# The last frame of a gated graph network: candidate product ahead of the update gate, the final update in pieces

## What is computed

```
a  = adj @ h                                   # in_mat and out_mat are both adj
z  = sigmoid([a, a] @ w3.T + b3 + h @ u3.T + bu3)
r  = sigmoid([a, a] @ w4.T + b4 + h @ u3.T + bu3)
hv = tanh([a, a] @ w5.T + b5 + (r * h) @ u5.T + bu5)
h  = (1 - z) * h + z * hv                      # three times
out = layernorm(x + h)                         # mean and variance over 256 features, no weights
```

## Time and profile before

| what | value |
|---|---|
| median of 3 runs | 763.11 us (762.76 to 763.23) |
| the profiled execution | 762.16 us |
| its span, first to last instruction | 760.4 us |
| PE busy | 747.4 us, 98% |
| DVE, ACT, POOL busy | 544.6 (72%), 388.3 (51%), 72.7 us (10%) |
| mean granted TensorE clock | 0.995 |

### The profile page before, as it was taken

The page is one execution under the profiler, slowest core; times in us unless marked ns, Lnnn a source line. Parts: engine busy times, 40 slices in busy tenths (PEclk is TensorE's granted clock), DMA queues, the critical chain, the costliest instruction groups (busy, mean ns, idle before and its releaser), DMA issues.

```text
span 760.4 us, 10506 instructions
## 1 busy us (share of the span) xinstructions
PE 747.4 (98%) x3696; PEld 633.4 (83%) x3696; DVE 544.6 (72%) x858; ACT 388.3 (51%) x647; POOL 72.7 (10%) x91
## 2 busy tenths in 40 slices
PE   9999999999999999999999999999999999999994
PEld 8888888888888888888888888888888888888883
DVE  5666787677767776787677766887677756887675
ACT  4545544455556453554556544545466545444454
POOL 0000021100110011110100001120000000211003
PEclk9999999999999999999999999999999999999998
DMA  8122411224453322223355332221335432212222
GB/s 308 29 38 38 91 29 31 38 41 87 114 121 65 88 58 35 37 38 58 66 121 119 85 91 32 38 35 30 68 64 130 128 67 37 32 31 32 42 39 112
DMA packets 208445, 52.15 MB, mean 69 GB/s; under 512 B 201232, under 2 KB 201360, under 8 KB 208400
## 3 DMA queue, kind: packets, MB, share of 16 engines
q1 hardware_dynamic: 208112, 51.23, 31.2%
q10 hardware_dynamic: 288, 0.27, 0.1%
HBM read 18.95 MB, written 8.39 MB: 36 GB/s over the span
## 4 chain that ended last, share of the span: by engine, by line
PE 98%; DVE 1%; ACT 0%; POOL 0%; issue 0%; ACTq 0%; POOLq 0%
PE ps_g L323 17%; PE ps_g L324 17%; PE ps_g L325 17%; PE ps_v L325 11%; PE ps_v L324 11%; PE ps_v L323 11%; PE ps_a L348 11%; PE ps_g L406 1%; DVE dz L609 0%; DVE hT L619 0%; DVE dz L604 0%; DVE hT_lo L635 0%; PE ps_a L445 0%; DVE stats L717 0%; POOL rstd L751 0%
## 5 line engine op out<-in xcount | busy, mean ns | idle before, releaser
L484 ACT ACTIVATE ps_v<-ps_v,bias 128x512 f32<-128x512 f32 x96 | 63.6, 663 | 200.3 <-PE ps_v L325 200.3
L325 PE MATMUL ps_g<-aT_hi,wt_hi 128*128 128x512 f32 x384 | 149.4, 389 | 0.0
L323 PE MATMUL ps_g<-aT_hi,wt_lo 128*128 128x512 f32 x384 | 149.4, 389 | 0.0
L324 PE MATMUL ps_g<-aT_lo,wt_hi 128*128 128x512 f32 x384 | 149.4, 389 | 0.0
L604 DVE TENSOR_TENSOR dz<-ps_v,hT 128x512 f32<-128x512 f32 x64 | 44.3, 692 | 103.6 <-ACT ps_v L484 103.6
L514 ACT CAST rh_hi<-rh 128x512 fp32r<-128x512 f32 x96 | 59.5, 620 | 78.2 <-DVE rh L624 78.2
L519 ACT ACTIVATE z<-ps_g,bias 128x512 f32<-128x512 f32 x96 | 64.2, 686 | 48.6 <-PE ps_g L325 48.6
L323 PEld LDWEIGHTS ps_g<-aT_hi,wt_lo 128*128 128x128 f32 x384 | 72.1, 188 | 15.0
L324 PEld LDWEIGHTS ps_g<-aT_lo,wt_hi 128*128 128x128 f32 x384 | 72.1, 188 | 15.0
L325 PEld LDWEIGHTS ps_g<-aT_hi,wt_hi 128*128 128x128 f32 x384 | 72.1, 188 | 14.9
L599 DVE TENSOR_TENSOR aT_lo<-ps_a,aT_hi 128x512 fp32r<-128x512 f32 x96 | 62.5, 674 | 28.8 <-ACT aT_hi L471 28.7
(11 more groups left out here) (60 smaller groups left out, 1169.1 us busy)
## 6 DMA issues: line engine op xcount, KB each, us to landing
hn<-hb SPq DMA_DIRECT2D x736, 32.0 KB, 2.0
x_in<-in_x_rows SPq DMA_DIRECT2D x16, 512.0 KB, 4.9
xT<-in_x_cols SPq DMA_DIRECT2D x15, 512.0 KB, 4.4
out<-y SPq DMA_DIRECT2D x15, 512.0 KB, 2.7
wide<-in_w_t SPq DMA_DIRECT2D x3, 512.0 KB, 6.2
xT<-in_x_cols SPq DMA_DIRECT2D x2, 256.0 KB, 4.3
out<-y SPq DMA_DIRECT2D x2, 256.0 KB, 2.0
square<-in_u_t ACTq DMA_DIRECT2D x1, 256.0 KB, 2.8
```

The costliest lines, as they stand in the source:

```text
L323: nc.tensor.matmul(dst, lhs_lo, rhs_hi, start=first, stop=False, skip_group_check=True)
L324: nc.tensor.matmul(dst, lhs_hi, rhs_lo, start=False, stop=False, skip_group_check=True)
L325: return nc.tensor.matmul(dst, lhs_hi, rhs_hi, start=False, stop=last, skip_group_check=True)
L484: nc.scalar.activation(ps_v[:, oc, :], ps_v[:, oc, :], ACT.Tanh, bias=bias[:, BV, oc:oc + 1]).then_inc(v_ready, 1)
```

## The change

In the last frame alone the order of work is another. PE runs the transposes of slot 2 right after `value`, then `candidate`, and `gate_z` last; to make that possible `gate_z` of frame 11 leaves `second_half`, and in the loop over rounds it stands at the head of the next pass. The update of frame 11 takes v-h of both chunks first; chunk 0 of z, of the product and of the sum stays whole, chunk 1 is made in two halves of 256 rows (two batches each). The transposes of slot 3 go by chunk and half, batches 0 and 1 into a bank of `ps_g[0]`, batch 2 and batch 3 into a bank of `ps_v` each. Slot 3 has an output tile of its own (`y_tail`); ACT scales batches 0, 1 and 2, DVE scales batch 3 by one `tensor_scalar`. The statistics of slot 1 come after those of slot 2 on DVE, and its scaling and its store after those of slot 2. On ACT z of the last frame comes after the first two batches of slot 2.

```diff
--- before.py
+++ after.py
@@ -114,6 +114,7 @@
         hb = [sb(f"hb{k}", [P, C, GB, QUADS, BLK]) for k in range(2)]
         z = [sb(f"z{k}", [P, C, ROWS]) for k in range(2)]
         y = [sb(f"y{k}", [P, GB, D]) for k in range(2)]
+        y_tail = sb("y_tail", [P, GB, D])
 
 
         hT_hi = sb("hT_hi", [P, C, ROWS], F32R)
@@ -190,6 +191,10 @@
         zd_ready = sem("zd_ready")
         h_ready = sem("h_ready")
 
+        tail_zpre, tail_z, tail_zd, tail_h = sem("tail_zpre"), sem("tail_z"), sem("tail_zd"), sem("tail_h")
+        tail_normed = [sem(f"tail_normed{hf}") for hf in range(2)]
+        tail_stored = sem("tail_stored")
 
 
         pool_passed, dve_passed = sem("pool_passed"), sem("dve_passed")
@@ -226,6 +231,14 @@
 
         def weight(k):
             return square[k - U3] if k in (U3, U5) else wsum[k]
+        def y_bank(q, b):
+            if q == SLOTS - 2:
+                return by_batch(ps_a[:, b // HB, :])[:, b % HB, :]
+            if b < HB:
+                return by_batch(ps_g[0][:, 0, :])[:, b, :]
+            return ps_v[:, b - HB, 0:D]
 
         block = ctx.enter_context(nc.Block())
 
@@ -305,15 +318,16 @@
             last = ROUNDS - 1
             for j in range(EARLY, FR - 1):
                 frame(last, j, True, False)
-            for q in range(SLOTS - 1):
+            for q in (0, 2, 1):
                 store(last, q)
             for hf in range(2):
                 part = slice(hf * HB, (hf + 1) * HB)
-                sp.wait_ge(normed[SLOTS - 1], GB * last + HB * (hf + 1))
+                sp.wait_ge(tail_normed[hf], HB)
                 sp.dma_start(out_rows[:, B - GB + hf * HB:B - GB + (hf + 1) * HB, :],
-                             y[1][:, part, :]).then_inc(stored[1], DMA)
+                             y_tail[:, part, :]).then_inc(tail_stored, DMA)
             sp.wait_ge(stored[0], DMA * (SLOTS // 2 * ROUNDS + 1))
-            sp.wait_ge(stored[1], DMA * (SLOTS // 2 * ROUNDS + 2))
+            sp.wait_ge(stored[1], DMA * (SLOTS // 2 * ROUNDS))
+            sp.wait_ge(tail_stored, DMA * 2)
 
 
         @block.tensor
@@ -387,7 +401,8 @@
 
                 gate_r(i, j)
                 value(i, j, carry)
-                gate_z(i, j)
+                if j < FR - 1:
+                    gate_z(i, j)
 
             def candidate(i, j):
 
@@ -431,6 +446,7 @@
 
             first_round()
             with nc.Fori(1, ROUNDS, engines=(pe.engine,), hint_back_edge=True) as i:
+                gate_z(i - 1, FR - 1)
                 first_half(i, 0, True)
                 candidate(i - 1, FR - 1)
                 for j in range(FR):
@@ -448,15 +464,29 @@
                         done.then_inc(y_transposed, 1)
 
             last = ROUNDS - 1
+            def last_output(c, hf):
+                for b in range(hf * HB, (hf + 1) * HB):
+                    done = nc.tensor.transpose(y_bank(SLOTS - 1, b)[:, c * P:(c + 1) * P],
+                                               hT[SLOTS - 1][:, c, b * N:(b + 1) * N], ident[:, :])
+                if c == C - 1:
+                    done.then_inc(y_transposed, 1)
             pe.wait_ge(a_lo_ready, 2 * frames(last, FR - 1))
             for c in range(C):
                 pe.wait_ge(h_ready, C * frames(last, FR - 2) - 1 + c)
                 output(SLOTS - 2, c, ps_a)
             candidate(last, FR - 1)
+            gate_z(last, FR - 1)
             pe.wait_ge(z_ready, C * frames(last, FR - 2))
-            for c in range(C):
-                pe.wait_ge(h_ready, C * frames(last, FR - 1) - 1 + c)
-                output(SLOTS - 1, c, ps_g[0])
+            pe.wait_ge(d_ready, C * frames(last, FR - 1))
+            pe.wait_ge(tail_h, 1)
+            for hf in range(2):
+                last_output(0, hf)
+            for hf in range(2):
+                pe.wait_ge(tail_h, hf + 2)
+                last_output(1, hf)
 
 
         @block.scalar
@@ -554,9 +584,22 @@
                 for j in range(FR - 1):
                     frame(i, j, True, (i, j + 1))
             last = ROUNDS - 1
-            frame(last, FR - 1, False, None)
-            tanh_v(last, FR - 1)
-            normalise(last, 1)
+            j = FR - 1
+            tanh_v(last, j - 1)
+            normalise(last, 0)
+            for oc in range(C):
+                act.wait_ge(rpre_ready, C * frames(last, j) - 1 + oc)
+                nc.scalar.activation(r_sb[:, oc, :], ps_g[1][:, oc, :], ACT.Sigmoid,
+                                     bias=bias[:, BR, oc:oc + 1]).then_inc(r_ready, 1)
+            for oc in range(C):
+                act.wait_ge(rh_ready, C * frames(last, j) - 1 + oc)
+                nc.scalar.copy(rh_hi[:, oc, :], rh[:, oc, :]).then_inc(rh_hi_ready, 1)
+            tanh_v(last, j)
+            def last_z(oc, rows):
+                act.wait_ge(zpre_ready, C * frames(last, j) - 1 + oc)
+                nc.scalar.activation(z[1][:, oc, rows], ps_g[1][:, oc, rows], ACT.Sigmoid,
+                                     bias=bias[:, BZ, oc:oc + 1]).then_inc(tail_z, 1)
 
             q = SLOTS - 2
             act.wait_ge(shift_ready[q], ROUNDS)
@@ -564,13 +607,18 @@
             for b in range(GB):
                 nc.scalar.activation(y[0][:, b, :], by_batch(ps_a[:, b // HB, :])[:, b % HB, :], ACT.Identity,
                                      bias=shift[q][:, b:b + 1], scale=rstd[q][:, b:b + 1]).then_inc(normed[q], 1)
+                if b == 1:
+                    last_z(0, slice(0, ROWS))
+                    for hf in range(2):
+                        last_z(1, slice(hf * HALF, (hf + 1) * HALF))
+            normalise(last, 1)
             q = SLOTS - 1
-            act.wait_ge(stored[1], DMA * turn(last, q))
-            for hf in range(2):
+            for hf, batches in enumerate(((0, 1), (2,))):
                 act.wait_ge(shift_ready[q], last + 1 + hf)
-                for b in range(hf * HB, (hf + 1) * HB):
-                    nc.scalar.activation(y[1][:, b, :], by_batch(ps_g[0][:, hf, :])[:, b % HB, :], ACT.Identity,
-                                         bias=shift[q][:, b:b + 1], scale=rstd[q][:, b:b + 1]).then_inc(normed[q], 1)
+                for b in batches:
+                    nc.scalar.activation(y_tail[:, b, :], y_bank(q, b), ACT.Identity,
+                                         bias=shift[q][:, b:b + 1], scale=rstd[q][:, b:b + 1])\
+                      .then_inc(tail_normed[hf], 1)
 
 
         @block.vector
@@ -708,26 +756,53 @@
                 for j in range(FR - 1):
                     frame(i, j, True, (i, j + 1))
             last = ROUNDS - 1
-            frame(last, FR - 1, True, None)
-
-            def last_statistics(q, src, hf):
+            j = FR - 1
+            v_minus_h(last, j - 1, 0)
+            times_z(last, j - 1, 0)
+            v_minus_h(last, j - 1, 1)
+            new_h(last, j - 1, 0)
+            times_z(last, j - 1, 1)
+            new_h(last, j - 1, 1)
+            for c in range(C):
+                times_r(last, j, c)
+            rh_low(last, j, 0)
+            rh_low(last, j, 1)
+            def last_statistics(q, hf):
 
                 dve.wait_ge(y_transposed, 2 * (q - (SLOTS - 2)) + hf + 1)
                 for b in range(hf * HB, (hf + 1) * HB):
-                    nc.vector.bn_stats(stats[q][:, b, :],
-                                       by_batch(src[:, hf, :])[:, b % HB, :]).then_inc(stats_ready[q], 1)
+                    nc.vector.bn_stats(stats[q][:, b, :], y_bank(q, b)).then_inc(stats_ready[q], 1)
                 dve.wait_ge(stats_ready[q], GB * last + HB * (hf + 1))
                 for b in range(hf * HB, (hf + 1) * HB):
                     nc.vector.bn_aggr(meanvar[q][:, b, :], stats[q][:, b, :]).then_inc(meanvar_ready[q], 1)
 
-            last_statistics(SLOTS - 2, ps_a, 0)
-            last_statistics(SLOTS - 2, ps_a, 1)
+            for hf in range(2):
+                last_statistics(SLOTS - 2, hf)
+            statistics(last, 1)
             for c in range(C):
-                v_minus_h(last, FR - 1, c)
-                times_z(last, FR - 1, c)
-                new_h(last, FR - 1, c)
-            last_statistics(SLOTS - 1, ps_g[0], 0)
-            last_statistics(SLOTS - 1, ps_g[0], 1)
+                v_minus_h(last, j, c)
+            def last_h(c, rows, nth):
+                dve.wait_ge(d_ready, C * frames(last, j) - 1 + c)
+                dve.wait_ge(tail_z, nth)
+                nc.vector.tensor_tensor(dz[:, c, rows], dz[:, c, rows], z[1][:, c, rows], ALU.mult).then_inc(tail_zd, 1)
+                dve.wait_ge(tail_zd, nth)
+                dve.wait_ge(xh_ready[SLOTS - 1], last + 1)
+                nc.vector.tensor_tensor(hT[SLOTS - 1][:, c, rows], dz[:, c, rows], xT[SLOTS - 1][:, c, rows],
+                                        ALU.add).then_inc(tail_h, 1)
+            last_h(0, slice(0, ROWS), 1)
+            for hf in range(2):
+                last_h(1, slice(hf * HALF, (hf + 1) * HALF), hf + 2)
+            q = SLOTS - 1
+            for hf in range(2):
```

(6 more changed lines are left out.)

## The result

The changed kernel took a median of 761.58 us (761.20 to 762.02, 19 runs) against 763.00 us before (762.19 to 763.41, 19 runs): 1.42 us less, a ratio of 0.9982 with a 95% interval of 0.9975 to 0.9988. It is faster, by 0.18%; the interval lies on both sides of the 0.2% that the prediction took as its line, so that line is neither reached nor missed. Forecast were 761.35 us in a range of 760.7 to 762.7.

A forecast was written before the change was run, and what follows sets the result against it. The body is bound by PE at work, so only the latency-bound tail can give time back. Earlier statistics, 1.30 us, plus one ACT batch less, 0.46, make 1.76 us: median 763.11 becomes 761.35 us, range 760.7 to 762.7.

The forecast's parts named there:

- Slot 2's transposes on PE: Last frame on PE: transposes start right after `value`, at 742.01 us instead of 744.74.
- I take nothing: Loop's edge on PE, crossed by `gate_z` of frame 11: no cost taken; from above 2.5 us at each of three edges.
- Statistics and scale of slot 2: DVE, then GpSimd: statistics run from 742.88 to 744.85 us, shift is ready at 746.76.
- z held back behind two batches: ACT: z of chunk 0 waits behind slot 2's first two batches, starting at 747.69, not 747.20; a 0.5 us wait.
- Times z: Last update on DVE: the product with z starts at 748.41 us.
- Halves at 0.42 us: DVE's chunk 1 update: each 256-column operation takes 0.42 us, on the line between 0.153 and 0.689.
- Statistics of slot 3: DVE after the update: they start at 751.32 us in place of 752.62, 1.30 us earlier.
- One batch less on ACT: Slot 3's scaling: ACT's last part is one batch, not two, saving 0.46 us.
- The end: Issue, transfer and completion of the last store after ACT's last batch: stays 2.52 us.
- halves at whole price: Rival on DVE's update: halves take 0.69 us each, gain only 0.68 us, median 762.4; chance 0.17.
- The hold at ACT: Rival: z of chunk 0 held longer, each 0.1 us delaying the end by 0.1; gain lost at 1.8 us; chance 0.06.
- The slower one: Rival: the loop's edge stalls PE at three edges; at 2.5 us each, median 768.9; chance 0.05.

The follow-up runs named there:

- the early edge: Changed kernel with `value` of frame 11 also moved to the head of the next pass, behind the loop for the last frame: 761.48 us, ratio 0.9981.
- the kernel with the whole chunk: Changed kernel with chunk 1 of the last update made whole again over 512 rows instead of in halves: 761.93 us, ratio 0.9989.

## Why the prediction was right, and where it was off

T was forecast at 18.58 - 1.76 = 16.82 and measured at 17.26, 16.95 in the kernel without the gap. Each time below is the forecast one moved by 0.62 for the later body, then the measured one.

1. *Slot 2's transposes on PE:* 742.63, measured 742.90. "I take nothing" for the loop's edge is the term that failed, 0.27 us. The edges between rounds are free, as forecast, though the earlier trace rows show it for the entry into the loop alone (190 us); the first branch back comes at 369.3 in the changed kernel. Behind that branch too `gate_z` follows `value` at the usual spacing (372.81 to 373.03, shown below the list). The gap is at the exit from the loop, which the prediction didn't look at. Before, the transposes stood straight behind the exit too, without a gap (744.51 to 744.74). There the instruction transfer of that moment starts at 739.68, 1.1 us ahead of the exit branch, and ends 3.65 us ahead of the last matmul; in the changed kernel, whose loop body has as many matmuls but begins and ends 12 matmuls earlier in PE's order, it starts 1.2 us behind the branch and ends 1 us ahead. Why it comes later stays open; the kernels with the early edge have no gap.
2. *Statistics and scale of slot 2:* 743.50 and 747.38, measured 743.81 and 747.69, late by that gap and 0.04 more. Their durations, 1.98 and 1.82, were right.
3. *z held back behind two batches:* 748.31, measured 748.64, late by what came before. In the kernel with the early edge, where there is no gap, z starts at 747.78, which is 747.70 on the time of the kernel before (0.08 for its later body); the forecast was 747.69. The new wait is real. Moving z ahead gave back 0.5 us; the prediction had 0.4, with DVE the next limit near 748.0. The product `gate_z` is next and DVE's own work close behind it: DVE waits 0.16 us.
4. *Times z:* 749.03, measured 749.43. From z's end to this start are 0.10 us where 0.03 were taken, the spacing of two engines in the earlier trace rows; DVE waits on two semaphores there. Only seen, not tested.
5. *Halves at 0.42 us:* 0.42 four times. The interpolation between 0.153 and 0.689 was right to the last digit. The Trainium skill, *VectorE: DVE Perf Modes*, "The TRN2 errata", has besides the formula weighed in the prediction another for fp32 `tensor_tensor`, (columns + 151) / 0.96 ns, which gives an estimated 0.424 for 256; the trace agrees with that one. Its advice against small pieces doesn't decide here: four pieces keep DVE 0.25 us longer than two whole ones (750.78 to 752.44 against 750.75 to 752.16) and still bring the end 0.46 nearer (some 0.36 at full clock), since PE can start on the first half.
6. *Statistics of slot 3:* 751.94, measured 752.37, so 0.87 us earlier than before and not 1.30. Of the 0.43 missing, 0.27 are the gap, 0.07 the spacing in point 4, and the rest 0.02 to 0.04 in three places.
7. *One batch less on ACT:* 0.46, measured 0.44 on the kernel before and 0.46 on the changed one with its gap taken off. DVE's batch had 0.85 us of room and used 0.54.
8. *The end:* 2.52 us from ACT's last batch, 757.15 to 759.67. Before they are 2.49 (757.88 to 760.37); the prediction's 2.52 came from the span rounded to 760.4. So nearly unchanged.

```profile
372.81 0.39 PE L339 MATMUL ps_v<-aT_hi,wt_hi 128*128 128x512 f32 x1
373.03 0.39 PE L337 MATMUL ps_g<-aT_hi,wt_lo 128*128 128x512 f32 x1
```

Of the rivals, halves at whole price fell (0.42). The hold at ACT did not get longer by itself, but its mechanism is how the gap reached the end: PE's 0.27 went through slot 2's statistics and scale into z, and each 0.1 there did cost 0.1; it was far from the 1.8 that would have lost the gain. The slower one had its mechanism on the right instruction and the wrong branch: nothing at the edges between rounds, 0.27 us once at the exit, too little to turn the result. And DVE's wait for z, which the forecast had at 0.4, was 0.65, with the gap and without it. The Trainium skill, *Runtime: NRT & Kernel Launch*, "Instruction fetch mechanics", says that a taken branch breaks the sequential prefetch. Here the two branches back, which are taken, cost PE nothing, and the gap stands behind the third, which leaves the loop. The branches are on PE's load queue, ahead of the matmuls. The columns are shortest, median and longest in ns and the first and last start in us, first of the kernel before, then of the changed one:

```profile
L433 PEldq COMPARE_BRANCH  x3: 88/442/889, 372.2 to 740.8; - x3
```

```profile
L448 PEldq COMPARE_BRANCH  x3: 88/228/261, 369.3 to 738.9; - x3
```

## What to carry to other kernels

When a tail runs by latency, write down for each step what stands ahead of it in its engine's queue: here an activation that the end hung on had been queued behind two batches of output that nobody waited for, and moving it was worth 0.47 to 0.5 us, as much as the shared scaling; shortening GpSimd's pass was worth 0.66. Look at PE's first instructions behind a loop's exit when code moves over the loop's edge. Where those are what the end hangs on, try a product in front of them: the three kernels that had one showed no gap. Compare a change of 0.2% by the stretch it touches, from a fixed instruction to the end of the span, which repeated to 0.02 us where whole executions spread by 0.8.

## What the runs showed that was not expected

- A gap of 0.27 us (four times) or 0.54 us (once) in front of the first instructions behind a loop's exit on PE, in five of the seven profiles with `value` as the loop's last product, and in none of the four where a product of 12 matmuls stood between. In the two profiles with `gate_z` as the last product there was none. Kernels with the same instructions on PE had 0, 0.27 and 0.54.
- The granted clock of PE fell from full level to half in every tail, after the last large matmul, and not at a fixed place: in the changed kernel at 752.48 in one profile and at 755.77 in another. The last group of transposes took 0.69 us in the first and 0.44 in the other (752.85), and T was 17.26 and 17.28, since nothing waited for that group. In the kernel with the whole chunk the fall hit a group that the end did wait for.
- A `tensor_scalar` of 128x256 fp32 from PSUM with two per-partition operands took 0.54 us on DVE, a `tensor_tensor` of the same size in SBUF 0.42, and an activation on ACT with scale and bias 0.56: the two engines are nearly even for such a batch.
